# Row maxima of past blocks and diagonal blocks taken apart, in an attention and expert kernel on one Trainium2 core

## The reference: what is computed

```python
scores = jnp.einsum('bhqd,bhkd->bhqk', q, k) / jnp.sqrt(jnp.float32(HD))
causal = jnp.tril(jnp.ones((s, s), bool))
scores = jnp.where(causal, scores, -jnp.inf)
attn = jax.nn.softmax(scores, axis=-1)
```

## Time and profile before

| | before |
|---|---|
| median of 3 runs | 715.46 us (714.61 to 715.82) |
| the profiled execution | 716.89 us, of which the span of instructions is 715.0 |
| mean granted clock of PE | 0.967 |
| PE busy | 631.5 us (88%) |
| PE weight loads | 384.0 us (54%) |
| DVE busy | 512.6 us (72%) |
| ACT busy | 395.2 us (55%) |
| POOL busy | 346.4 us (48%) |
| row-maximum reduces (L1397) | 352, 216.4 us when overlaps are taken off |
| score products of the maxima (L864) | 503 in the trace, of 512 |
| mask products of the maxima (L868) | 329 in the trace, of 352 |

### The profile page before, as it was taken

One profiled execution on the slowest core, in us unless ns is written; L12 is line 12 of the kernel. 1 busy time (PEld: TensorE's weight loads), 2 busy tenths in 40 slices (PEclk: granted clock), 3 DMA queues, 4 the chain that ended last, 5 costly groups with the idle time before them and its releaser, 6 DMA issues.

```text
span 715.0 us, 15200 instructions
## 1 busy us (share of the span) xinstructions
PE 631.5 (88%) x4753; PEld 384.0 (54%) x4806; DVE 512.6 (72%) x1712; ACT 395.2 (55%) x794; POOL 346.4 (48%) x390
## 2 busy tenths in 40 slices
PE   7987699899999999999999999898977879999990
PEld 3534356556646656654665665455544446666660
DVE  7364957777896897788689688668767265447994
ACT  3234256567556656755665575475445365566771
POOL 4042264157259266634916654263212357656783
PEclk9999999999999999999999999999989898999996
DMA  6201001000100110010011010001601114334543
GB/s 172 72 0 31 1 1 30 1 1 1 44 22 1 31 35 1 5 52 9 1 30 35 1 29 28 11 2 43 200 9 34 50 45 124 92 112 143 163 151 97
DMA packets 40218, 34.18 MB, mean 48 GB/s; under 512 B 6673, under 2 KB 37329, under 8 KB 40129
## 3 DMA queue, kind: packets, MB, share of 16 engines
q1 hardware_dynamic: 35824, 23.84, 12.5%
q0 software_dynamic: 4320, 9.38, 3.8%
HBM read 17.54 MB, written 12.57 MB: 42 GB/s over the span
## 4 chain that ended last, share of the span: by engine, by line
PE 49%; DVE 21%; POOL 15%; issue 9%; ACT 3%; SPq 1%; DMA 0%; DVEq 0%; POOLq 0%; ACTq 0%
PE wide L1090 8%; DVE nmax L1397 7%; PE small L864 5%; PE small L909 5%; PE wide L884 4%; PE small L896 3%; PE small L930 3%; PE small L1106 3%; PE small L959 3%; PE small L1097 2%; POOL k_rows L1310 2%; PE small L868 2%; PE wide L889 2%; DVE a_xn L1389 2%; DVE a_st L1378 2%
## 5 line engine op out<-in xcount | busy, mean ns | idle before, releaser
L1397 DVE TENSOR_REDUCE nmax<-small 128x1 f32<-128x512 f32 (+3 forms) x352 | 216.4, 637 | 50.5 <-PE small L868 42.7
L1194 ACT ACTIVATE pT<-wide 128x1024 f32<-128x1024 f32 x160 | 159.2, 1022 | 57.3 <-PE wide L889 56.2
L864 PE MATMUL small<-kz,qT 128*128 128x256 bf16 (+3 forms) x503 | 123.2, 306 | 14.4 <-DVE nmax L1397 13.8
L1326 POOL DMA_INDIRECT token_rows<-m_row,place_u x64 | 62.8, 981 | 119.3 <-DVE place_u L1611 90.3
L884 PE MATMUL wide<-qT,kz 128*128 128x128 bf16 (+3 forms) x491 | 92.7, 299 | 10.0 <-DVE qT L1548 8.6
L1335 POOL DMA_INDIRECT result_rows<-k_rows,dest x71 | 70.2, 988 | 46.3 <-issue 24.8
L909 PE MATMUL small<-pT,v_pad 128*5 128x512 f32 (+3 forms) x1024 | 78.8, 449 | 1.1 <-issue 1.1
L868 PE MATMUL small<-future_sb,idb 128*128 128x128 bf16 (+2 forms) x329 | 78.3, 238 | 0.6
L1090 PE MATMUL wide<-kz,a_work 128*128 x142 | 74.4, 606 | 0.0
L864 PEld LDWEIGHTS small<-kz,qT 128*128 128x128 bf16 x512 | 44.3, 99 | 48.9 <-DVE nmax L1397 30.5
L884 PEld LDWEIGHTS wide<-qT,kz 128*128 128x128 bf16 x512 | 43.6, 98 | 42.3 <-issue 10.0
(11 more groups left out here) (249 smaller groups left out, 1268.2 us busy)
## 6 DMA issues: line engine op xcount, KB each, us to landing
a_qkv_sb<-token_rows SPq DMA_DIRECT2D x71, 72.0 KB, 1.9
kz<-k_all SPq DMA_DIRECT2D x32, 128.0 KB, 2.4
x<-L_attn_x SPq DMA_DIRECT2D x8, 256.0 KB, 3.6
kz<-L_ffn_w SPq DMA_DIRECT2D x2, 1024.0 KB, 7.6
kz<-result_rows SPq DMA_DIRECT2D x16, 128.0 KB, 2.3
out<-x SPq DMA_DIRECT2D x16, 128.0 KB
result_rows<-k_rows,dest POOLq DMA_INDIRECT x71, 2.3
token_rows<-m_row,place_u POOLq DMA_INDIRECT x64
```

Of the source, the lines that this page charges most:

```text
L864: pe.matmul(bank[:, at:at + keys], qT1[:, m.parity, g, tile * P:(tile + 1) * P], kz[:, m.parity, g, r, 0:keys], start=(r == r0), stop=Fals ...
L1194: act.activation(pT[:, g % 2, s, :], wide[:, w % 2, :], ACT.Exp, scale=SCALE_B)\
L1326: pool.indirect_dma_start(token_rows[:, :], bass.IndirectOffsetOnAxis(ap=place_u[:, n, t:t + 1], axis=0), m_row[:, n, t, :], None).then_in ...
L1397: ins = dve.tensor_reduce(nmax[:, tile, g * R + r0:g * R + r0 + heads], bank[:, 0:heads * (tile + 1) * P].rearrange("p (h k) -> p h k", h= ...
```

## The change

MAX_JOBS gets a fourth entry, whether a job is of diagonal blocks. Seven jobs of past blocks alone come first: tile 3 by single heads over keys 0 to 383, tile 2 by two heads over 0 to 255, tile 1 by all four heads over 0 to 127. They need no mask. Then four jobs, one a tile from 3 down to 0, of the diagonal 128 keys of all four heads, with the mask. A job has one score product for all its heads, and a diagonal job one mask product. Past maxima go to a new tile `past_max`, diagonal ones to `nmax`, and m_cut takes the minimum of both (both are negated) for tiles 1 to 3 and waits for it on a new semaphore before it goes on. A group still has 11 jobs, and the steps' order is as before.

```diff
-MAX_JOBS = [(3, r, 1) for r in range(R)] + [(2, r, 1) for r in range(R)] + [(1, 0, 2), (1, 2, 2), (0, 0, R)]
+MAX_JOBS = ([(3, r, 1, False) for r in range(R)] + [(2, r, 2, False) for r in range(0, R, 2)] + [(1, 0, R, False)]
+            + [(tile, 0, R, True) for tile in (3, 2, 1, 0)])
...
+        past_max = sb("past_max", [P, NT - 1, H])
...
+        whole_max = sem("whole_max")
...
             def max_job(m, ring, g, n):
                 job = max_name(g, n)
-                tile, r0, heads = MAX_JOBS[n]
-                keys = (tile + 1) * P
+                tile, r0, heads, diagonal = MAX_JOBS[n]
+                lo, hi = (tile * P, (tile + 1) * P) if diagonal else (0, tile * P)
...
-                for r in range(r0, r0 + heads):
-                    at = (r - r0) * keys
-                    pe.matmul(bank[:, at:at + keys], qT1[:, m.parity, g, tile * P:(tile + 1) * P],
-                              kz[:, m.parity, g, r, 0:keys], start=(r == r0), stop=False, skip_group_check=True)
-
-                diagonal = bank[:, 0:heads * keys].rearrange("p (h k) -> p h k", h=heads)[:, :, keys - P:keys]
-                last = pe.matmul(diagonal, idb[:, :], future_sb[:, 0:heads, :], start=False, stop=True,
+                last = pe.matmul(bank[:, 0:heads * (hi - lo)], qT1[:, m.parity, g, tile * P:(tile + 1) * P],
+                                 kz[:, m.parity, g, r0:r0 + heads, lo:hi], start=True, stop=not diagonal,
                                  skip_group_check=True)
+
+                if diagonal:
+                    last = pe.matmul(bank[:, 0:heads * P], idb[:, :], future_sb[:, 0:heads, :], start=False, stop=True,
+                                     skip_group_check=True)
                 full(ring, job, last)
...
-                ins = dve.tensor_reduce(nmax[:, tile, g * R + r0:g * R + r0 + heads],
-                                        bank[:, 0:heads * (tile + 1) * P].rearrange("p (h k) -> p h k", h=heads),
-                                        AX, ALU.max, negate=True)
+                to = nmax[:, tile, :] if diagonal else past_max[:, tile - 1, :]
+                ins = dve.tensor_reduce(to[:, g * R + r0:g * R + r0 + heads],
+                                        bank[:, 0:heads * (1 if diagonal else tile) * P]
+                                        .rearrange("p (h k) -> p h k", h=heads), AX, ALU.max, negate=True)
                 empty(ring, job, ins)
...
                         if g:
                             dve.wait_ge(small_free[ring.bank(last_max)], ring.count(last_max))
+                        dve.tensor_tensor(nmax[:, 1:NT, heads], nmax[:, 1:NT, heads], past_max[:, :, heads], ALU.min)\
+                           .then_inc(whole_max, 1)
+                        dve.wait_ge(whole_max, G * m.n + g + 1)
                         high = nmax[:, :, :].bitcast(BF16).rearrange("p t (h two) -> p t h two", two=2)[:, :, heads, 1]
                         dve.tensor_tensor(slot[:, :, :, 1], mx, high, ALU.subtract)
```

## The result

The changed kernel takes 733.17 us (median of 4 runs, 731.61 to 734.17) where the kernel before took 715.04 us beside it; the ratio is 1.0256, with an interval of 1.0237 to 1.0274. It is 18 us slower, where 4.5 were forecast, and outside the range (713 to 725). The span of the profiled execution is 729.7 us against 715.0, 14.7 us more. The profiled execution of before (716.89 us) lies 1.9 us over its median and that of after (731.61 us) 1.6 under its own, which is why the two traces differ by less than the two medians.

What follows compares the result with a forecast made beforehand. PE was taken as nearly full, idle where it waits for DVE, no engine alone setting the end. Cuts +5.0, order 0 and products -0.5 made +4.5 us: 720.0 us on the 715.46 us median, range 713 to 725.

Steps and rivals of the forecast that it cites:

- The products: Score and mask products on PE: same 7168 columns per group, 384 fewer products in all, taken as -0.5 us.
- Rival (b): Weight loads set PE's pace, so fewer products of 128 columns free it: 702.8 us, or an estimated 710; chance 0.03.
- The reduces: Row-maximum reduces on DVE: 7.00 us a group before, 7.02 after, nothing in the sum; still near 219 us in total.
- The cut: Added minimum and its wait in each m_cut on DVE: 0.20 us each, 3.6 to 6.4 us exposed, taken as +5.0.
- POOL takes no part: POOL's chain has 2.3 us of slack before p_k0 for a later a_qkv3, so it adds nothing.
- The order: Lighter front and heavier back of each group on PE and DVE: taken as 0, bounds 3.4 us either way.
- the return: In the walk through one iteration, the p_x jobs give back 0.4 us on PE in front of a_r.
- The cut's exposure: PE's shift weight loads wait for the cut at 18 of 32 groups: wait up from 12.2 us by 3 or more.
- (d): Jobs 7 to 10 collide in the two-bank ring; PE's bank waits well over 30 us: 726.3 us; chance 0.12.

Runs made afterwards that it cites:

- the minimum alone: Kernel before, each cut also taking a minimum of nmax with itself (128x12) and waiting for it; jobs and products unchanged: 726.26 us, ratio 1.0146.
- the reversed order: Changed kernel with the four diagonal jobs of a group first and the seven past jobs after them, minimum kept in the cut: 729.02 us, ratio 1.0193.
- the order alone: Changed kernel without the minimum and its wait, past maxima unused, exponentials at a quarter of the scale: 720.53 us, ratio 1.0065.
- early or late minimum: Early: changed kernel, minimum behind job 9's reduce, 728.23 us. Late: kernel before, minimum added behind the cut's copy into an unread tile, 718.05 us.
- the 32 waits: 32 more already satisfied waits near DVE's start: changed kernel 759.3 us, again 761.41 us; kernel before 752.8 us, again 753.37 us.
- the quarters: Changed kernel with both of p_cut's POOL subtractions issued as four of a quarter width: 729.18 us, ratio 1.0187; same in kernel before: 714.85 us.

## Why the prediction was wrong

**The products: right.** Same columns, PE's busy time within 1.1 us, one product a job without effect. Rival (b), which had a chance of 3%, did not come.

**The reduces: right.** 218.7 us, forecast at near 219.

**The cut: right in its own size, wrong in what it sets off. This is the step that failed most.** "I take 0.20 us" stands: the minimum of group 3 starts at the place of the old subtraction and puts it 0.20 us later (0.19 and 0.20 us at cut 0 and cut 1 of the run with the minimum alone). The sum then multiplied 0.20 by 18 to 32. At cut 2 the price is 0.98 us, in each of the table's five iterations, since the two operations behind the minimum run into POOL's 1.16 us subtraction. "POOL takes no part", the prediction says, because its chain has 2.3 us of slack; that it could hold DVE was not weighed. Two signs were in the profile of before: the cut's subtraction had a mean of 290 ns over 32 with a median of 230, and its 0.58 us in group 2 ended with POOL's cast. The Trainium skill (SBUF — State Buffer, Who interferes with whom) states it: a VectorE instruction with two SBUF inputs, or a copy in a mode that uses both ports, and a GpSimd instruction that reads SBUF exclude each other for a whole instruction, while a reduce never contends. The traces agree: the held ones are the subtraction (1.23 us), the copy (1.16 us) and the minimum (0.33 us), all within 0.1 us of POOL's end, and the reduces of the same stretch keep 0.68 us. With that wait in it the term of the cut would have been 3.6 to 6.4 us and, by the rows, an estimated 1 us for each of seven or eight cuts of group 2: 11 to 14 instead of 5. The run with the minimum alone gave 10.7, but that is in part luck: 3.1 of it is the stall at the loop's end, and without it some 7 are left, fewer than the estimate, since cut 3 gives 0.23 us of an iteration back. Of an iteration the prediction wanted 0.4 to 0.8 us more as its sign; it is 1.75, and 1.15 with the minimum alone.

**The order: put at 0, and it costs 5 us.** "It closes near 0. I take 0" was the walk through an iteration. With the maxima apart and no minimum an iteration is 0.68 us longer: 0.41 at cut 1, 0.31 at cut 3, nothing at cuts 2 and 0; 5.0 us over the program (3.3 to 6.0 by the interval), where the bound was 3.4. The mechanism was named (lead lost in a wait, back half in full), and the reversed order shows it at cut 1. What failed is the return: the 0.4 us that the p_x jobs were to give back in front of a_r do not show at cut 0 (13.69 against 13.72).

**The cut's exposure: right in direction, too small.** The waits of the shift's weight loads for the cut were to grow from 12.2 us by 3 or more. They are, in after's list of waits (waiting engine, tile and line, the releaser, then us in all, cases, the longest in us):

```profile
PEld small L1012 <- DVE q_rows L1550: 29.2, 31, 3.3
```

17 us more, and at 31 of the 32 groups in place of 18. The forecast's direction is right. The two runs that part the causes have 25.0 us here (the minimum alone) and 16.1 us (the order alone), which is 12.8 and 3.9 more than before and adds up to the 17. So the row holds both causes: 0.2 us in most cuts, 1 us at each cut 2, the 3.3 at the loop's end, and some of the order's.

**Not foreseen: the stall at the loop's end.** 2.9 us of the 15.3 in the traces. No row of before had it in that place (its own stall of 1.6 us lay in front of L1382, in the same iteration, and cost about 1 us of cut 1's gap there, 15.37 instead of 14.3). The runs with the minimum alone and with the reversed order have 3.1 us there, the ones without or with an early or late minimum do not have it or have it elsewhere. That it hangs on the instructions' places is shown by the 32 waits. The traces also hold DMA packets of the kind "instruction", which the page of after counts by queue (packets, MB, share of 16 engines):

```profile
q8 instruction: 40, 0.66, 0.4%
q14 instruction: 30, 0.25, 0.1%
```

These are packets of 16 KB and of 8 KB. In front of the minimum behind the loop DVE stood from 455.43 to 458.42, and a packet of queue 14 ran from 456.54 to 457.07. Over all the kept traces, 16 of the 17 stalls of DVE of this kind (over 1.2 us, "issue", between 75 and 575 us) have a packet of queue 14 that ended 1.28 to 1.63 us before DVE went on, and the trace of after has only 16 such packets in its first 570 us. So DVE most likely waits for its own instructions; no run changed the packets alone, and what decides the places was not tried. The Trainium skill (Runtime: NRT & Kernel Launch, Instruction fetch mechanics) says that each engine's instructions are fetched in blocks by a queue of their own. These packets agree with that, though their records do not name the engine.

**The rivals.** (d), collision in the back half, came nearest in time (726.3), and its sign came true: PE's waits for emptied banks went from 30.5 us to 42.7 (23.5 and 19.2, by tile), in 90 cases. They are the order's: with the minimum alone they are 31.4 us, with the order alone 44.2. But (d) cannot hold more than the order's 5.0 us, the larger loss is the cut's, and with the order reversed the waits are still 41.5 us though cut 1 comes 0.7 us sooner. How much of the 5.0 us is PE waiting for a bank, and how much the lost lead, no run tells apart. Sum of the parts against the median's 18.1 us: 10.7 for the run with the minimum alone (some 7 for it and what it sets off, 3.1 for the stall), 5.0 for the order, 2.4 for both together or uncertain by the intervals of the two runs (about 2 us each). PE's clock has little part in it: its mean is 0.965 after and 0.967 before, over the spans some 2 us of full speed at most. After such a stall the granted clock falls for some us (busy us of PE, PEld, DVE, ACT, POOL, then the clock, in the stretch behind the loop's end):

```profile
462.00:470.00 8.00, 8.00 (x60) 4.11 (x59) 4.15 (x17) 4.54 (x5) 1.04 (x1) 0.71 0.01 2
```

0.71 is a stretch partly at 1.2 GHz; PE had stood some 3 us before it.

## What to carry to other kernels

An operation added on DVE costs what it shifts, not only what it lasts: look at what POOL runs in the microsecond after, and at any small DVE operation whose mean lies above its median, before a price is put on 0.2 us. Work that is equal in sum and only moved toward the end of a group was not free here, where something waits behind its end. Compare distances between the same events, iteration by iteration: those of cut 2 and cut 3 of one kernel agreed to some 0.1 us between iterations and between sessions, where the totals of one kernel moved by 2 to 7 us within a session and by 37 between sessions; a distance that does not agree, as that of cut 0, shows where to look. And read a run's total only beside its trace: two totals here (the minimum alone and the quarters) fitted a forecast in part because a stall of 2 to 3 us had come or gone elsewhere.

## What the runs showed of the hardware

A copy of 16 bf16 numbers a partition on DVE took 0.19 us alone and 1.16 us when POOL had started a two-input subtraction of 512 fp32 numbers 0.07 us before it; with that subtraction cut in four pieces no operation of the cut lasted longer than 0.69 us, held by a cast of 0.61. Reduces from PSUM were not held: of 128x512 numbers they took 0.68 to 0.69 us with POOL's subtraction under them (14 in the trace of after) and without. At a loop's jump or end an engine stood 1.6 to 3.7 us with nothing to wait for that the profile shows (DVE 2.99, PE 3.73), and 32 instructions more in front moved DVE's stall to another place. The same kernel took 715 us in some sessions and 750 to 753 us in others. In the changed kernel 10.3 us of such a difference lay before the last cut, mostly at the borders between iterations (cut 0 after 15.3 instead of 13.87 us), and 16.5 us in the experts' part; a ratio of 1.0256 in the one became 1.0119 in the other.
